# A fused attention and expert-mixing layer on one core: the output bias on the returned residual as one GpSimd operation, one slot earlier

## The reference

```python
q = heads(x @ Wq + bq); k = heads(x @ Wk + bk); v = heads(x @ Wv + bv)   # 16 heads of 16
qp = relu(q @ rw) + EPS; kp = relu(k @ rw) + EPS                         # 64 features a head
kv = kp^T v;  qkv = qp kv;  norm = qp . sum(kp)
x = layernorm(x + (qkv / (norm + EPS)) @ Wo + bo)
sim = routing scores of (x @ Wrq) with the keys       # 4 heads, 2 halves, 64 keys each
sx, sy = top 8 of each half; scores, idx = top 8 of sx + sy (of 64 x 64 pairs)
w = silu(x . down_embed[idx]) * softmax(scores)
mlp = (silu(x @ Wg + bg) * (x @ Wu + bu)) @ Wd + bd
x = layernorm(x + mlp + sum(w * up_embed[idx]))
```

## Time and profile before

| | |
|---|---|
| median of 3 runs | 3481.85 us |
| lowest and highest | 3479.89 and 3484.04 us |
| the profiled execution | 3480.97 us |
| its span, first to last instruction | 3479.1 us |
| around the span | 1.9 us |
| PE, DVE, ACT, POOL busy in the span | 3362.4, 2870.6, 1991.4, 1301.9 us |
| granted TensorE clock over the span | 0.989 |
| chain that ended last | PE 82%, DVE 7%, ACT 6%, POOL 2% |

### The profile page before, as it was taken

How to read it: one execution, slowest core, us unless ns; L and a number is a source line. 1 busy time by engine, 2 the same in 40 slices (tenths; PEclk the granted TensorE clock), 3 DMA queues, 4 the chain that set the end, 5 groups by cost and what they waited for, 6 DMA issues and landing times.

```text
span 3479.1 us, 48605 instructions
## 1 busy us (share of the span) xinstructions
PE 3362.4 (97%) x17888; PEld 2641.6 (76%) x17888; DVE 2870.6 (83%) x5316; ACT 1991.4 (57%) x2886; POOL 1301.9 (37%) x788
## 2 busy tenths in 40 slices
PE   8779999999999999999999999999999999999988
PEld 6457877777777777877777877777877777777767
DVE  4688878988888888888888887888888888888873
ACT  4456556555556555566556566556556565555541
POOL 0234333334333434343334343344333344434441
PEclk9889999999999999999999999999999999999999
DMA  4000000100001000000001000100000000000000
GB/s 122 25 19 31 19 19 31 31 25 31 19 19 31 31 25 31 19 19 31 31 25 31 19 19 31 31 25 31 19 19 31 31 19 25 25 19 25 13 19 19
DMA packets 36762, 94.35 MB, mean 27 GB/s; under 512 B 6832, under 2 KB 11184, under 8 KB 36528
## 3 DMA queue, kind: packets, MB, share of 16 engines
q1 hardware_dynamic: 36528, 91.25, 8.2%
HBM read 57.68 MB, written 33.55 MB: 26 GB/s over the span
## 4 chain that ended last, share of the span: by engine, by line
PE 82%; DVE 7%; ACT 6%; issue 3%; POOL 2%; DMA 0%; SPq 0%; POOLq 0%; ACTq 0%; DVEq 0%
PE ring L672 26%; PE y_bank L757 11%; PE y_bank L759 11%; PE step_bank L574 6%; PE step_bank L566 5%; PE step_bank L672 4%; PE step_bank L610 3%; PE step_bank L602 3%; PE step_bank L701 3%; PE step_bank L691 3%; PE step_bank L745 3%; DVE prob L1160 2%; PE step_bank L560 2%; POOL grid L479 1%; ACT prob L911 1%
## 5 line engine op out<-in xcount | busy, mean ns | idle before, releaser
L479 POOL TENSOR_TENSOR grid<-ex 128x1024 f32<-128x1024 f32 x512 | 994.5, 1950 | 1469.6 <-ACT ex L892 726.5
L757 PE MATMUL y_bank<-wd_sb,gate 128*128 128x256 f32 x2048 | 622.8, 386 | 9.2 <-DVE wexp L1182 9.2
L759 PE MATMUL y_bank<-up_sb,wexp 128*128 128x256 f32 x2048 | 613.3, 381 | 0.0
L1160 DVE SCALAR_TENSOR_TENSOR prob<-grid,narrow,prob 128x1024 f32<-128x1024 f32 x256 | 580.2, 2266 | 9.0
L672 PE MATMUL ring<-x1T_hl,downT_hl 128*128 128x512 f32 x1536 | 421.2, 410 | 23.8 <-ACT gate L917 23.7
L672 PE MATMUL ring<-x1T_hl,wg_hl 128*128 128x512 f32 x1536 | 430.1, 415 | 5.0 <-DVE gate L1176 5.0
L759 PEld LDWEIGHTS y_bank<-up_sb,wexp 128*128 128x128 f32 x2048 | 391.8, 191 | 54.2
L1147 DVE SCALAR_TENSOR_TENSOR grid<-grid,best 128x1024 f32<-128x1024 f32 x256 | 343.6, 1342 | 107.0 <-POOL grid L479 105.1
L672 PE MATMUL ring<-x1T_hl,wu_hl 128*128 128x512 f32 x1536 | 421.2, 409 | 0.0
L757 PEld LDWEIGHTS y_bank<-wd_sb,gate 128*128 128x128 f32 x2048 | 362.0, 192 | 70.8 <-issue 37.9
L672 PEld LDWEIGHTS ring<-x1T_hl,wu_hl 128*128 128x128 f32 x1536 | 281.9, 188 | 119.6 <-issue 42.9
(11 more groups left out here) (168 smaller groups left out, 5551.2 us busy)
## 6 DMA issues: line engine op xcount, KB each, us to landing
xb<-in_L_attn_x SPq DMA_DIRECT2D x34, 512.0 KB, 4.2
x_kept<-x SPq DMA_DIRECT2D x32, 512.0 KB, 5.1
prob<-x_kept SPq DMA_DIRECT2D x32, 512.0 KB, 3.6
out_y<-x SPq DMA_DIRECT2D x32, 512.0 KB, 2.7
xa<-in_L_attn_x SPq DMA_DIRECT2D x30, 512.0 KB, 3.5
prob<-in_L_ffn_down_embed SPq DMA_DIRECT2D x1, 1024.0 KB, 6.2
prob<-in_L_ffn_Wg SPq DMA_DIRECT2D x1, 1024.0 KB, 10.0
prob<-in_L_ffn_Wu SPq DMA_DIRECT2D x1, 1024.0 KB, 10.7
```

The source lines that it names most:

```text
L479: pool.tensor_tensor(grid[:, h % 2], bcast(ex[:, h, 0:NX].unsqueeze(2), [P, NX, NK]), bcast(ex[:, RH + h, 0:NK].unsqueeze(1), [P, NX, NK]) ...
L757: pe.matmul(rows, gate[:, c % 2, t * P:(t + 1) * P], wd_sb[:, c, :], start=(c == 0 and t % 2 == 0), stop=False, skip_group_check=True)
L759: mm = pe.matmul(rows, wexp[:, c % 2, t * P:(t + 1) * P], up_sb[:, c, :], start=False, stop=(c == C - 1), skip_group_check=True)
L1160: ins = dve.scalar_tensor_tensor(out=row, in0=g, scalar=rz[:, h:h + 1], in1=row, op0=ALU.mult, op1=ALU.add, accum_out=mass[:, 0:1] if h == ...
```

## The change

The two additions of 512 elements at the end of slot 5 become one over both stretches, in slot 4 ahead of `spread(2, 0)`. It raises `res_bias` by one, and DVE waits for that count. The wait for `res_loaded` moves with it.

```diff
@@ body of POOL, loop over c
                     if at and c == 6:
                         norm_scale(at_dve, (m + 1) * AT_STEPS, ln1_pool, m, mv1, rstd1, rstd1_ready)
+                    if ff and c == C // 2:
+                        pool.wait_ge(res_loaded, (n + 1) * 16)
+                        rows = residual(par).rearrange("p i (t d) -> p i t d", t=2)
+                        pool.tensor_tensor(rows, rows, bcast(bd_sb[:].unsqueeze(1).unsqueeze(1), [P, 2, 2, D]),
+                                           ALU.add).then_inc(res_bias, 1)
                     if rt and not odd:
                         spread(t, 0)
                     kv_adds(KV_LATE[c])
                     if rt and not odd:
                         spread(t, 1)
-                    if ff and c == 5:
-                        pool.wait_ge(res_loaded, (n + 1) * 16)
-                        rows = residual(par).rearrange("p i (t d) -> p i t d", t=2)
-                        for i in range(2):
-                            pool.tensor_tensor(rows[:, i], rows[:, i], bcast(bd_sb[:].unsqueeze(1), [P, 2, D]),
-                                               ALU.add).then_inc(res_bias, 1)
@@ y_rows() of DVE
-                    dve.wait_ge(res_bias, (f + 1) * 2)
+                    dve.wait_ge(res_bias, f + 1)
```

## The result

The changed kernel takes 3496.16 us (median of 6 runs, 3494.41 to 3498.57), the kernel before 3480.86 us on the same chip (6 runs, 3476.09 to 3484.04). The ratio is 1.0045 with a 95% interval of 1.0033 to 1.0057: slower by 15.3 us. The forecast was 3482.9 us and no change, with a range up to 3487 us. The time lies outside it. The profiled execution of the changed kernel took 3498.57 us, its span is 3496.8 us, which is 17.7 more than before. Behind the edit every line number is one lower than before (L1147 of DVE is now L1146, L1160 is L1159; of ACT L856 is L855; of PE L701 is L700); the new addition is L503. `kp` are the keys' features, which ACT evacuates from a PSUM bank (L856 before, L855 now).

The account below looks back on a forecast made before the run. PE was taken to bound the middle and the chain through routing the tail. Tail +1.0 us (5 x (+2.13 - 1.93)), middle and moved wait 0, on 3481.85 gave about 3482.9 us, range 3478 to 3487.

Parts of the forecast that it names:

- How POOL and DVE disturb each other: Slots 3 and 5: two-input DVE instructions and POOL's SBUF operations exclude each other for a whole instruction; spread's wait 1.75 us.
- H: Slot 4: time the merged 1024-element addition holds DVE's L1147, taken as 2.36 - 0.23 = 2.13 us.
- The tail's sum: Five tail iterations: +2.13 us in slot 4, -1.93 in slot 5, +0.20 each, +1.0 us together.
- The moved wait: POOL's wait for res_loaded in slot 4: over 4 us before it is reached, so it costs nothing.
- The middle iterations: 26 iterations: DVE 1.6 us late in slot 4, gains 1.36 in slot 5; PE never notices, 0 us.
- What covers the delay: Middle, slot 5: PE's gate product has 3.1 us of cover, its third product 2.7 us, against 1.6 us delay.
- This second one: Middle, slot 5: PE's third product, needing ACT's gate, is late next, with 2.7 us of cover.
- The sum: Whole kernel: +1.0 us, all from the tail, with 0 from the middle.
- The slow operation: Slot 4 rival: larger H costs the tail, then beyond 2.7 us cover every middle iteration; 3523 us at H = 4.3; 6 in 100.

Follow-up runs that it names:

- run 7: The changed kernel with POOL's one addition in slot 4 held back until DVE has closed tile 1 (its clamp): 3471.86 us, 0.9970 against the kernel before.

## Why the prediction was wrong

- **How POOL and DVE disturb each other: right.** H, the hold of the addition on DVE, was forecast as 2.13 us and is 2.13 in the tail; L1146 in the middle takes 2.82 against 2.9 forecast. The size of H came by analogy, from what one addition of 512 holds less than it lasts, and it could have missed by some tenths. The rule of the Trainium skill (SBUF — State Buffer, "Who interferes with whom") is borne out by a third operation, and by run 7, in which the addition stood beside the maxima, which read PSUM, and neither was held.
- **The tail's sum: right.** +0.20 us an iteration was forecast, +0.20 to +0.26 came in the three full ones, 1.2 us in all against +1.0. The merge brings all of it; the move gives the tail back in slot 5 what it takes in slot 4, and one operation holds 0.2 us more than two.
- **The moved wait: right.** L503 waits for the load in iteration 37 alone. DVE waits nowhere for the sum.
- **The middle iterations: this step failed.** Its size of the delay was right (1.6 forecast, 1.59 measured). What failed is "What covers the delay", which named ACT's gate with 2.7 us and said "This second one is what is late next." Late next is ACT's evacuation of `kp`, which follows the exponential directly in ACT's order, and the bank it frees for PE's L701, with 1.2 us. I followed the data from DVE (L1176, the gate) and not the queue of ACT, where the delayed exponential pushes back what has nothing to do with routing; in the rows of ACT I went from L892 to L917 past the instruction between them. With 1.2 in that place the step would have read 1.6 - 1.2 = 0.4 us in PE, and 26 x 0.4 = 10 us at most. The runs give 18 x 0.36 = 6.5 us, because the six iterations directly behind the end of a sequence lose nothing, nor do the middle's first and last (6 and 31). Behind an end ACT is 0.6 us earlier to begin with: in iteration 28 of the kernel before, `kp` is out 16.67 us behind L407 and PE wants the bank at 18.52, a cover of 1.85 us, and the delay there is 1.54.
- **The clock: not foreseen.** The granted clock of 1.00 in the middle was taken as given, and it was not asked whether a late PE could lose it. In three profiles each, 4.3 stretches on average after against 0.7 before: 3.7 x 1.7 = 6.3 us.
- **The sum.** Bank 6.5, clock 6.3, tail 1.2: 14.0 of 15.3 us. The other 1.3 us I can't place; single executions differ by more than that ahead of the first L407.
- **The rivals.** The slow operation did not come (2.40 us alone); but its second half, that a delay beyond the cover counts in every middle iteration, is what happened, with less than half of the cover stated. It had 6 in 100, for a threshold of H = 3.2; with the right cover the threshold is 0.5 + 1.2 = 1.7 us, below the H that I had just worked out. The whole prediction of the middle hung on that one cover.

## What to carry to other kernels

When work on one engine is delayed, list what stands behind the delayed instruction in each in-order queue that it reaches, evacuations of PSUM banks above all, and take the shortest cover of the list, not that of the next step of the same data. If a loss is found, changing the order in that queue can be enough (here ACT's `kp` ahead of the exponential gave back all of the loss in the middle), and moving a second engine's SBUF work to where the first one reads PSUM can give more (here 11 us against the kernel before). A wait table names only the idle part of such a loss; the distance from iteration to iteration shows all of it.

## What the runs showed of the hardware

- A two-stretch addition of 1024 elements on POOL takes 2.36 to 2.40 us alone, like one stretch of 1024 (L466, 2.36), and holds a two-input instruction of DVE for 2.13 us. Beside DVE's maxima out of PSUM it takes 2.36 us and they stay at 1.14 us for eight.
- TensorE's granted clock fell to 0.50 (1.2 GHz) for 3.4 us right behind sixteen matmuls of 33x33, with PE busy for 38.84 of the 38.90 us ahead of the fall in iteration 11. It did so at 5, 3 and 5 of seven ends of sequences in three profiles of the changed kernel and at 1, 0 and 1 in three of the kernel before; each fall cost 1.7 us. The same sixteen matmuls stand at every end, in the kernel before at 19 of 21 without a fall. The Trainium skill (TensorE: Matmul & The Clock Gate, section "HAM oscillation — how this bites in real kernels") tells of the clock falling where PE waits for data; the rows here show no such wait at that place, so this case does not bear that out as the only way for it to fall.
- Fifteen scalings of one element a partition take 1.51 us on ACT back to back and eight 0.86 us, 0.10 us each, while the group by line gives a mean of 0.19 us for one: so such short instructions overlap, and a mean duration can't be multiplied by their number.
